# Eight-batch mixture and attention kernel: weights prepared on TensorE, the zero fill moved, the last gathers without spacing powers

## The reference

```python
x = x + 0.5 * ffn(layernorm(x))        # 8 experts, top 2 of a router, relu, biases
x = x + attention(layernorm(x))        # 16 heads of 8, causal, rotary positions
x = x + 0.5 * ffn(layernorm(x))        # the same experts again
x = x + 0.5 * quantised(layernorm(x))  # blocks of 32 rounded to a 6 bit grid, times a weight
x = x + gated(layernorm(x))            # tanh/sigmoid gates, a scan over time, silu ffn
x = x + 0.5 * quantised(layernorm(x))
# ffn: out = sum over the top two experts e of gate_e * (relu(x W1[e] + b1[e]) W2[e] + b2[e])
```

## Time and profile before

| | us |
|---|---|
| median of 3 runs | 979.24 |
| lowest, highest | 977.0, 981.04 |
| profiled execution | 978.61 |
| its span, first to last instruction | 976.8 |
| PE busy | 837.3 (86%) |
| POOL busy | 666.3 (68%) |
| DVE busy | 623.6 (64%) |
| ACT busy | 550.1 (56%) |

### The profile page before, as it was taken

How to read it: one execution, slowest core, us unless ns; L and a number is a source line. 1 busy time by engine, 2 the same in 40 slices (tenths; PEclk the granted TensorE clock), 3 DMA queues, 4 the chain that set the end, 5 groups by cost and what they waited for, 6 DMA issues and landing times.

```text
span 976.8 us, 23169 instructions
## 1 busy us (share of the span) xinstructions
PE 837.3 (86%) x7489; PEld 615.0 (63%) x7489; DVE 623.6 (64%) x1918; ACT 550.1 (56%) x1221; POOL 666.3 (68%) x851
## 2 busy tenths in 40 slices
PE   2279568987999999999999999999997998757884
PEld 2279568963856576564557555668975997434553
DVE  7650016267589687789978977884435346597674
ACT  2234234436576767666766767677663556744751
POOL 6728996788894337888741897884599983786342
PEclk9999869998999999999999999999998999776897
DMA  8958446583844343453444353433532771110000
GB/s 316 331 209 237 126 130 182 172 225 105 232 141 120 98 136 111 139 157 97 136 116 134 89 152 111 127 92 99 170 111 90 218 219 41 35 28 33 1 11 32
DMA packets 117271, 129.65 MB, mean 133 GB/s; under 512 B 14883, under 2 KB 84643, under 8 KB 117030
## 3 DMA queue, kind: packets, MB, share of 16 engines
q1 hardware_dynamic: 108966, 111.39, 38.8%
q0 software_dynamic: 8192, 16.79, 5.9%
HBM read 87.37 MB, written 40.37 MB: 131 GB/s over the span
## 4 chain that ended last, share of the span: by engine, by line
PE 36%; POOL 34%; DVE 12%; issue 8%; ACT 6%; DMA 3%; SPq 1%; POOLq 0%; DVEq 0%; ACTq 0%
PE bank L765 32%; POOL small L1642 10%; POOL z_scratch L1651 8%; POOL yg L1664 7%; PE bank L777 4%; POOL P L1686 4%; DVE sm_m L1277 2%; DMA yg<-y_scratch,pos 2%; POOL sm_f L1621 1%; ACT P L1441 1%; ACT P L1523 1%; DVE xs L1215 1%; POOL ab L1674 1%; DMA z_scratch<-P 1%; DVE xs L1218 1%
## 5 line engine op out<-in xcount | busy, mean ns | idle before, releaser
L1277 DVE TENSOR_REDUCE sm_m<-bank 128x4 f32<-128x512 f32 (+2 forms) x320 | 204.8, 682 | 52.3 <-PE bank L765 49.6
L1523 ACT ACTIVATE P<-bank 128x512 f32<-128x512 f32 x320 | 173.8, 596 | 32.9 <-PE bank L765 27.3
L765 PE MATMUL bank<-w2r,hb 128*128 x1360 | 188.5, 283 | 0.0
L765 PE MATMUL bank<-zt,wt 128*128 128x128 f32 x1360 | 181.5, 284 | 4.3 <-ACT zt L1466 3.4
L1686 POOL TENSOR_SCALAR_AFFINE_SELECT P<-P 128x256 f32<-128x256 f32 (+1 forms) x320 | 116.1, 383 | 96.4 <-ACT P L1523 92.6
L765 PEld LDWEIGHTS bank<-zt,wt 128*128 128x128 f32 x1360 | 166.6, 197 | 13.4 <-issue 4.8
L1651 POOL DMA_INDIRECT z_scratch<-zb,pos x128 | 131.6, 1028 | 59.5 <-issue 24.6
L765 PEld LDWEIGHTS bank<-w2r,hb 128*128 128x128 f32 x1360 | 166.2, 193 | 2.6 <-issue 0.7
L1482 ACT ACTIVATE hb<-bank 128x512 f32<-128x512 f32 x170 | 100.9, 596 | 96.2 <-PE bank L765 83.3
L1642 POOL TENSOR_TENSOR small<-small 128x4 f32<-128x4 f32 x137 | 145.4, 1061 | 10.6 <-DVE pos L1201 7.2
L1664 POOL DMA_INDIRECT yg<-y_scratch,pos x128 | 130.6, 1020 | 23.7 <-issue 20.7
(11 more groups left out here) (219 smaller groups left out, 1407.6 us busy)
## 6 DMA issues: line engine op xcount, KB each, us to landing
wt<-w_scratch SPq DMA_DIRECT2D x170, 256.0 KB
zin<-z_scratch SPq DMA_DIRECT2D x82, 128.0 KB
y_scratch<-yt SPq DMA_DIRECT2D x82, 128.0 KB
q_scratch<-qpart SPq DMA_DIRECT2D x48, 128.0 KB
k_scratch<-kpart SPq DMA_DIRECT2D x48, 128.0 KB
Ks<-k_scratch SPq DMA_DIRECT2D x64, 96.0 KB
Qs<-q_scratch SPq DMA_DIRECT2D x64, 96.0 KB
z_scratch<-P SPq DMA_DIRECT2D x6, 512.0 KB, 5.7
```

What stands on the lines that cost most here:

```text
L765: return e.matmul(o, lhs, rhs, start=start, stop=stop, **kw)
L1277: e.tensor_reduce(to, of, AX.X, ALU.max, negate=True).then_inc(*d_max.step(i, f"m{s_}"))
L1523: e.activation(P[:, (2 * i + s_) % PR, :], shared("scor", i, 0, s_), ACT.Exp, scale=SCALE).then_inc(*a_sc.step(i, f"e{s_}"))
```

## The change

- `LATER_FILL` begins with the buffer of phase 1, and is issued at the end of `late` instead of behind the sixth `zin`. Phase 1's scatters are planned after `late`.
- wr is no longer sent. W1 goes in whole, and PE multiplies it with a matrix `less` (identity with -1 in the last row's place) into a bank; ACT copies the bank back over W1. SP writes 127 rows per expert, and the biases go by one DMA of their own into the last rows of w_scratch.
- `begin` becomes a planned stage; batch 1 is the second DMA instead of the sixth; one more constant (`less`) is loaded.
- ACT does a small Exp at its very start.
- `route` multiplies and reduces both choices in one step each (o1 and o2 lie in one tile), and the expert numbers `ei` become a step of their own behind the positions.
- Scatters of phase 0 and gathers of the last phase are planned 1.35 apart (`ROWS_CLOSE`), all other row moves 2.2 as before. A pause is only put where calls would be nearer than that less 0.25, so none is left in these two places.

The core of the diff:

```diff
-LATER_FILL = pieces_of(0, PHASE[0].blocks * SB, SLOTS) + pieces_of(1, 0, SLOTS)
+LATER_FILL = pieces_of(1, 0, SLOTS) + pieces_of(0, PHASE[0].blocks * SB, SLOTS)
...
-    "sload": ("S0.95+6",
+    "begin": ("S0.9+2.6 S0.47+2.6<-1 S1.9+2.4<-1 S1.9+2.7<-1 S0.47+2.3<-1 S0.02+0.0<-1",
             [], 1),
-    "split": ("G1.25 S0.52+4",
+    "sload": ("S0.47+4.5",
             [], 1),
+    "split": ("P0.97+0.2 A0.6+0.15 S0.52+4",
+            [(0, 1)], 1),
...
-    "route": ("P0.2+0.2 D4.9+0.15",
+    "route": ("P0.2+0.2 D3.3+0.15 D1.1+0.15",
             [(0, 1)], 1),
...
-ROWS_APART, ROWS_CALL = 2.2, 1.15
+ROWS_CLOSE, ROWS_APART, ROWS_CALL = 1.35, 2.2, 1.15
...
-        return [("route", OF_TILE[u], 1)] if k == 0 else []
+        return [("route", OF_TILE[u], 1)] + ([("late", 0, 0)] if OF_TILE[u] == 1 else []) if k == 0 else []
...
-def moves_rows(stage, u, k):
-
-    return k < 2 and (stage == "scat" and OF_TILE[u] > 0 or stage == "comb")
+def moves_rows(stage, k):
+
+    return k < 2 and stage in ("scat", "comb")
+
+
+def apart(stage, u):
+
+    return ROWS_CLOSE if (stage, OF_TILE[u]) in (("scat", 0), ("comb", PHASES - 1)) else ROWS_APART
...
-                if between + ROWS_CALL < ROWS_APART - 0.25:
+                if between + ROWS_CALL < apart(stage, u) - 0.25:
...
                 e.dma_start(wout[:, :, :], a["wout"]).then_inc(l_late, 16)
+                fill(LATER_FILL, l_zero)
                 yield
...
                 e.dma_start(P[:, n, :], a["w1"][n]).then_inc(l_raw[n], 16)
-                e.dma_start(last_row(n), a["wr"][n]).then_inc(l_raw[n], 16)
                 if n == NE - 1:
+                    e.dma_start(wd.rearrange("(e r) c -> e r c", r=128)[:, D - 1, :], a["b1"]).then_inc(s_w, 16)
                     fill(FIRST_FILL, l_zero0)
...
-                w.wait_ge(*p_split.at(n, "w"))
-                e.dma_start(wd[128 * n:128 * n + 128, :], P[:, n, :]).then_inc(s_w, 16)
+                w.wait_ge(*a_split.at(n, "w"))
+                e.dma_start(wd[128 * n:128 * n + D - 1, :], P[0:D - 1, n, :]).then_inc(s_w, 16)
...
-                if n == 5:
-                    fill(LATER_FILL, l_zero)
...
+            def split(n):
+                w.wait_ge(l_less, 16)
+                w.wait_ge(l_raw[n], 16)
+                o = take("split", n, 0, a_split.at(n, "w"))
+                mm(o, less_last, P[:, n, :], True, True).then_inc(*t_split.step(n, "w"))
+                yield
...
-                for k, oh in ((1, o1), (2, o2)):
-                    then(e.tensor_tensor(by_j(m_), oh[:, 0:T, :], by_j(ps), ALU.mult), f"m{k}")
-                    then(e.tensor_reduce(pf[:, k - 1, :], by_j(m_), AX.X, ALU.add), f"p{k}")
+                then(e.tensor_tensor(m_, oh[:, :, 0:T, :], by_j(ps).unsqueeze(1).to_broadcast([128, 2, T, 8]), ALU.mult), "m")
+                then(e.tensor_reduce(pf, m_, AX.X, ALU.add), "p2")
                 then(e.tensor_copy(pos[:, f % 2, :, 0:T], pf), "pos")
+                yield
...
+            def split(n):
+                w.wait_ge(*t_split.at(n, "w"))
+                e.activation(P[:, n, :], shared("split", n, 0), ACT.Copy).then_inc(*a_split.step(n, "w"))
+                yield
...
+            w.wait_ge(*d_init.at(0, "half"))
+            e.activation(early, mhalf, ACT.Exp)
...
-                w.wait_ge(l_raw[n], 32)
-                e.tensor_tensor(P[:, n, :], P[:, n, :], last_row(n), ALU.subtract).then_inc(*p_split.step(n, "w"))
```

More of the change, by code:

```diff
@@ L184, in follows @@
 def follows(stage, u, k):
-    if stage in ("first", "sload"):
+    if stage == "begin":
         return []
+    if stage == "first":
+        return [("begin", 0, 2 + k)]
+    if stage == "sload":
+        return [("begin", 0, 5)]
+    if stage == "wquant":
+        return [("begin", 0, 3)] if k == 0 else []
     if stage == "xload":
@@ L214, in follows @@
     if stage == "bias":
-        return [("first", 0, 1)] if k == 0 else []
+        return [("first", 0, 1), ("begin", 0, 4)] if k == 0 else []
     if stage == "res":
@@ L254, in network @@
 def network():
-    counts = {"first": 1, "xload": NB - 2, "late": 1, "sload": NE, "split": NE, "wquant": 1, "prep": 2 * NB, "route": PHASES, "scat": NTILE,
+    counts = {"begin": 1, "first": 1, "xload": NB - 2, "late": 1, "sload": NE, "split": NE, "wquant": 1, "prep": 2 * NB, "route": PHASES, "scat": NTILE,
               "bias": 1,
@@ L346, in forward @@
         free[engine] = start + steps[k][1]
-        if moves_rows(stage, u, k):
-            free["R"] = start + ROWS_APART
+        if moves_rows(stage, k):
+            free["R"] = start + apart(stage, u)
         done[stage, u, k] = free[engine] + steps[k][2]
@@ L385, in backward @@
         free[key[2]] = left[x] = end + plan[x[0]][0][x[2]][1]
-        if moves_rows(*x):
-            free["R"] = end + ROWS_APART
+        if moves_rows(x[0], x[2]):
+            free["R"] = end + apart(x[0], x[1])
         del known[key]
@@ L706, in wload @@
                 if u == 0:
[L707 removed]
+                    w.wait_ge(s_w, 16 * (NE + 1))
                 if u >= WR:
@@ L752, in mxb @@
                 yield
-            begin()
-            follow("S", {"sload": sload, "split": split, "xload": xload, "late": late, "wload": wload, "zin": zin, "res": res, "proj": proj, "stack": stack,
+            follow("S", {"begin": begin, "sload": sload, "split": split, "xload": xload, "late": late, "wload": wload, "zin": zin, "res": res, "proj": proj, "stack": stack,
                          "mrow": mrow, "mxb": mxb})
@@ L1047, in gated @@
                 yield
-            follow("P", {"prep": prep, "route": route, "zin": zin, "hid": hid, "res": res, "proj": proj,
+            follow("P", {"prep": prep, "split": split, "route": route, "zin": zin, "hid": hid, "res": res, "proj": proj,
                          "maxi": maxi, "mrow": mrow, "scor": scor, "val": val, "heads": heads, "wquant": wquant,
```

65 lines of the change are left out of this document (36 added, 29 removed), and 2 rows, old and new, of the table STAGES.

## The result

The changed kernel takes **1028.14 us** (median of 4 runs, 1026.62 to 1029.77) against 978.38 of the kernel before beside it (977.0 to 981.04): ratio **1.0505**, 95% interval 1.0473 to 1.0538. Forecast were 958.7 us and a range of 947 to 968. The kernel is slower by 5%, by a mechanism that was none of the rivals.

A forecast was written before the change was run, and what follows sets the result against it. TensorE was taken as the bound from 250 to 700 us, with POOL's chain ahead of it. 978.6-17.0 (start)-0.5 (routing)-3.0 (last gathers) = 958.1, with 0.6 for the median 958.7 us; range 947 to 968.

The forecast's parts named there:

- This is ahead of the positions as worked out next, so the fill leaves the path: Load stage: 15.5 MB moved by the end of the later zero fill, 48 us, before phase 1's positions at 54.9.
- It is wrong if the zero fill still ends last: Sign against the forecast: phase 1's scatters, forecast near 55 us, should wait for positions and not for the zero fill.
- Rival (4): Gathers without a power ahead wait for the one before; from 1.1 us per call slower by 0.5%; chance 0.03.
- Rival (1): Start gains only 10 to 12: half-clock products or phase 0's blocks waiting for expert weights; 963 to 968; chance 0.14.
- The table load: Start, ACT: an early Exp takes the 1.28 us load from in front of the first normalisation; logits end at 14.3.
- seven split products: Start, PE: seven fp32 products ahead of the counting product, taken as 7 us, between 6.1 and 12.1 at half rate.
- Start, 17.0 us: Phase 1's first scatter at about 55.1 instead of 72.05, 17.0 us earlier; 18 with fast products, 12 at halved clock.
- Gathers of phase 0: POOL, behind phase 1's scatters: start moves from 127.49 to 110.5 us, PE's gap shrinks from 17 to about 3.
- just met: Second limit on phase 0's gathers: PE's block results stored by 109 to 111 us, hid starting 2 to 3 earlier.
- Middle, 0: All six phases replanned; PE idles 12.4 us of 450 there; taken as 0, and 6 us either way.
- rival (5): The middle gives back 8 to 12 us by a worse order of attention work; 967 to 971; chance 0.08.
- Last phase's gathers, 3.0: End of kernel, POOL: seven entries fewer between first and last gather; ends -7.9 and +2.8 us, 3.0 gain taken.

The follow-up runs named there:

- fix128_again: Repeat run of the changed kernel with all eight split-weight stores writing 128 rows, b1 rows written behind them; 962.37 us, ratio 0.9843.
- fix128: Changed kernel with the eight split-weight stores writing 128 rows instead of 127, b1 rows written behind them; 967.94 us, ratio 0.988.
- b_fill: Kernel before with only the later zero fill moved to the end of the load stage; 970.43 us, ratio 0.9925.
- b_close: Kernel before without the five spacing powers between the last phase's gathers; 975.88 us, ratio 0.9986.
- b_both: Kernel before with the later fill at the end of the load stage and no spacing powers between the last phase's gathers; 969.27 us, ratio 0.9917.
- b127: Kernel before with its eight split-weight stores writing 127 rows, the rows 127 by one small transfer; 1047.08 us, ratio 1.0713.
- fix_far: fix128 with seven spacing powers put back between the last phase's gathers; 965.41 us, ratio 0.9872.
- fix_far_again: Repeat run of fix128 with seven spacing powers put back between the last phase's gathers; 963.44 us, ratio 0.9859.
- two112: Changed kernel with each 127-row store split into transfers of 112 and 15 rows; 966.41 us, ratio 0.9879.
- two124: Changed kernel with each 127-row store split into transfers of 124 and 3 rows; 971.96 us, ratio 0.9926.
- fix_fill6: fix128 with the later zero fill put back behind the sixth read of z_scratch; 972.33 us, ratio 0.995.

## Why the prediction was wrong

**The step that failed** is the one that is not there. The forecast costed the products and the ACT copies of the split, and the new place of the fill, but the write that follows them stood in no sentence. The plan kept its 0.52 us (`S0.52+4` in both versions of `split`), although the rows of the transfer changed from 128 to 127. It cost a median of 10.12 us instead of 0.51, in eight stores and the entry behind them 80.2 us, on the queue whose next entries are the late weights and the fill. "This is ahead of the positions as worked out next, so the fill leaves the path" rested on 325 GB/s for all bytes of the start. The stores were 2 MB of these, and they went at 26 GB/s. "It is wrong if the zero fill still ends last" is what happened: POOL waited 68.1 us for it. The Trainium skill would have shown it before the run, by the section named above; it was not weighed.

**Rivals.** None named SP. Rival (4), slower by the gathers, had the right sign and the wrong place: the last phase's gathers took 1.06 us on average, against 1.07 before. Rival (1), 10 to 12 us at the start and 963 to 968 in all, has the size that the versions without slow stores show, but not by its conditions: the seven products did not run at half clock throughout, and no product of phase 0 waited for expert weights in fix128_again.

**Steps that held**, in the changed kernel itself. The table load ran at 0.79 and the logits ended at 10.70+3.42 = 14.1 (forecast 14.3); seven split products took 7.7 us (7), the first two more than 1 us each and the others 0.86, the full-clock price, as the ACT copies behind them show (16.07, 17.44, 18.30, 19.16, 20.02); the counting product ran at 21.53 (21.3), positions came at 25.06 (24.7):

```profile
0.79 1.28 ACT L1643 ACT_TABLE_LOAD   x1 [0.79 <-PEq L1854]
...
10.70 3.42 PE L781 MATMUL bank<-rwt,pb 128*128 128x8 f32 x16
13.98 7.72 PE L781 MATMUL bank<-P,tb 128*128 128x512 f32 x14
21.53 0.19 PE L781 MATMUL bank<-cb,tri 128*128 128x64 bf16 x1
...
24.89 0.17 DVE L1224 CAST pos<-rs 128x16 uint32<-128x16 f32 x1
```

**Terms that were mis-sized**, read where the stores are out of the way:

- *Start, 17.0 us.* The scatters of phase 1 started at 58.54 in fix128_again, 13.5 earlier than in the earlier trace rows, and at 59.68 in fix128. In order of time, fix128_again:

```profile
42.45 1.04 POOL L1653 TENSOR_TENSOR sm_p<-sm_p,small 128x4 f32<-128x4 f32 x1
...
43.58 0.87 DVE L1124 BATCH_NORM_STATS2 sm_p<-xs 128x6 f32<-128x128 f32 x4
...
44.97 0.15 DVE L1139 SCALAR_TENSOR_TENSOR sm_p<-sm_p 128x4 f32<-128x4 f32 x1
...
58.54 1.15 POOL L1678 DMA_INDIRECT z_scratch<-zb,pos  x1 [2.63 <-DVE pos L1225]
```

 The power of batch 4 ran at 42.45, not 40.6; 1.1 of this was there at the first scatter of phase 0 (26.14, where 27.81-2.8 = 25.0 was forecast). The step that uses its result (L1139) came 2.5 us later and not 1.1 as in the kernel before (45.91 to 47.01), since batch 5's statistics now stand in front of it on DVE. 1.85 and 1.4 are the 3.4 us between 55.1 and 58.54 but for 0.2. In fix128 gaps of 0.5 and 1.1 us between DVE's own steps for batch 4 came on top, unexplained. I had followed POOL's list and taken DVE's as unchanged.
- *Gathers of phase 0.* They started at 117.34 in fix128_again and 117.35 in fix128, 10.1 us earlier, whether the scatters had started at 58.54 or 59.68. What sets it is the end of PE's block work, the limit that the prediction called "just met". This work ends at 109.8, inside the 109 to 111 worked out, but in part by luck: its first products began at 62.00, 1.1 later than in the kernel before (60.94) and not 2 to 3 earlier, because PE waited 2.1 us for a preparation in front of them; they ended 0.3 earlier, having no wait for expert weights between (1.0 before). PE's next products are logits. DVE marks two batches with them and takes statistics, and a power that stands in front of the gathers waits for these (fix128_again):

```profile
109.69 1.85 PE L782 MATMUL bank<-rwt,pb 128*128 128x8 f32 x16
...
111.70 1.03 POOL L1678 DMA_INDIRECT z_scratch<-zb,pos  x1 [0.20 <-issue]
...
115.84 0.17 DVE L1134 TENSOR_SCALAR sm_p<-sm_p 128x4 f32<-128x4 f32 x1
...
116.11 1.04 POOL L1653 TENSOR_TENSOR sm_p<-sm_p,small 128x4 f32<-128x4 f32 x1 [3.37 <-DVE sm_p L1134]
117.34 1.02 POOL L1691 DMA_INDIRECT yg<-y_scratch,pos  x1 [0.20 <-issue]
```

- *Middle, 0.* From the gathers of phase 0 to those of the last phase it took 699.1 us before, and 697.9, 702.5, 698.9 and 698.7 in b_fill, b_close, b_both and b127, which keep that order. With the new order it took 699.1 in the changed kernel, 706.9 in fix128, 698.2 in fix128_again, 701.8 in fix_far, 699.9 in fix_far_again, 703.2 in two112, 704.1 in two124 and 697.7 in fix_fill6. The means are 699.4 and 701.3, with 8.7 between two runs of the same kernel, so the new order costs some 2 us or nothing. After fix128 alone I took this for rival (5), the middle giving back 8 to 12; the same kernel run again, with 698.2, speaks against it.
- *Last phase's gathers, 3.0.* The section shrank by 7.7 to 8.2 in the versions without powers, the upper end that I had worked out (7.9), and 1 to 3.3 of it came back behind the last gather (91.5 us from there to the end in fix128_again, 88.3 before). I took 3.0 since a step waiting for DVE stood in the section; the new order has that step elsewhere.

For fix128_again the terms are -10.2 (phase 0's gathers), -0.9 (middle), -8.2 (section), +3.2 (behind it): -16.0, span 960.8 against 976.8. The forecast was -20.5. Without the slow stores the kernel ends inside the range of 947 to 968, if only just in the first set of runs (967.94, then 962.37 us by the medians), with the biggest term of the sum 7 too large and the gathers' term 2 too small.

## What to carry to other kernels

When a transfer changes shape, cost it anew, and look at the divisors of its row count before its bytes: one row fewer can take a transfer from 16 engines to one. A slow transfer costs most where it is queued first, on the queue that also issues what the critical path needs next. And where a step is said to come earlier, follow the list of every engine that it passes, not only of the one that was late before.

## What the runs showed of the hardware

Slow transfers block the engine that issues them, and not from the first on: SP was through the first 254 KB store of 127 rows in 0.29 us, then held a median of 10.12 per store, and 10.09 at the transfer of `w2r` behind them. The empty 30 us of the changed kernel had 26 GB/s in all. Stores of 124 and 3 rows took 2.6 us a pair, of 112 and 15 rows about 1.0, of 128 rows 0.9 (eight in 7.31 us).

The granted clock makes two runs of one kernel differ in a place that has nothing to do with the change. Two stretches of PE between 370 and 610 us, fix128 and then fix128_again (stretch, us, busy, granted clock, DMA share, GB/s):

```profile
370.00:400.00 30.00, 28.23 (x311) 0.94 0.49 141
...
580.00:610.00 30.00, 26.96 (x282) 0.89 0.40 111
```

```profile
370.00:400.00 30.00, 28.90 (x336) 1.00 0.51 148
...
580.00:610.00 30.00, 27.28 (x317) 1.00 0.52 132
```

PE was idle 1.8 and 3.0 us of these stretches in fix128 and 1.1 and 2.7 in the repeat. Where the granted clock is 0.94 and 0.89, a part of the stretch ran at 1.2 GHz instead of 2.4. Over the whole middle, from phase 0's gathers to the last phase's, PE was busy 673.6 us in fix128 (6540 records, mean granted clock 0.97) and 665.9 us in the repeat (6537, 0.98): the same work took PE 7.7 us longer, which is most of the 8.7 us between the middles. Whole executions show it too: of the 23 of the kernel before beside fix128_again, the shortest (970.12 us) had a mean granted clock of 0.961, the longest (982.97) 0.944. The gathers of phases 0 and 1 stood at the same time in both profiles (222.38 and 222.60), those of phase 2 were 4.8 us apart (400.91 and 396.14), those of phase 3 6.7 (586.94 and 580.25), of phase 4 9.7 (748.29 and 738.58). One profile of a kernel bound by PE is therefore no measure of a middle section to better than some 8 us. What lowers the clock in one run and not in the other stays open.
